# Score products in three float32r parts instead of float32, with a shifted schedule of the attention stage

## What is computed

```
scores = einsum('bhid,bhjd->bhij', Q, K) / scale
QJ     = einsum('bhid,hde->bhie', tanh(Q), J_attn)
scores = scores + lambda_attn * einsum('bhie,bhje->bhij', QJ, tanh(K))
scores = where(causal, -inf, scores)
out    = einsum('bhij,bhjd->bhid', softmax(scores), V);   x = x + out @ Wo.T + bo
```

## Time and profile before

| | |
|---|---|
| median of 3 runs | 2140.23 us (2136.80 to 2142.74) |
| the profiled execution | 2137.79 us, span 2136.1 us |
| PE busy | 1957.2 us, 92% of the span |
| DVE, ACT, POOL busy | 1246.5, 1065.7, 820.6 us |
| attention, routing with shared expert, experts (about) | 0 to 1165, to 1500, to 2136 us |
| granted PE clock, mean | 0.983 |

### The profile page before, as it was taken

The page is one execution under the profiler, slowest core; times in us unless marked ns, Lnnn a source line. Parts: engine busy times, 40 slices in busy tenths (PEclk is TensorE's granted clock), DMA queues, the critical chain, the costliest instruction groups (busy, mean ns, idle before and its releaser), DMA issues. The chain is left out here.

```text
span 2136.1 us, 48445 instructions
## 1 busy us (share of the span) xinstructions
PE 1957.2 (92%) x14755; PEld 1296.5 (61%) x14824; DVE 1246.5 (58%) x3875; ACT 1065.7 (50%) x2310; POOL 820.6 (38%) x1206
## 2 busy tenths in 40 slices
PE   2689999999999999999988999997999999999997
PEld 1345445454454544545435788886777777777776
DVE  5666667766667666776662865553445545444553
ACT  1255555555555555555552345452555555555553
POOL 4033323333323333233332037773444444444443
PEclk9799999999999999999999999999999999999999
DMA  7234443344443434434322346654863333333332
GB/s 240 60 106 117 121 136 124 110 118 119 136 130 107 122 111 140 128 114 124 100 87 79 137 134 226 223 188 150 215 167 58 57 55 55 56 55 57 54 57 34
DMA packets 156641, 246.08 MB, mean 115 GB/s; under 512 B 29408, under 2 KB 90592, under 8 KB 156480
## 3 DMA queue, kind: packets, MB, share of 16 engines
q1 hardware_dynamic: 120960, 189.24, 28.9%
q0 software_dynamic: 32064, 53.44, 12.2%
q10 hardware_dynamic: 3456, 1.34, 0.3%
HBM read 111.89 MB, written 90.50 MB: 95 GB/s over the span
## 5 line engine op out<-in xcount | busy, mean ns | idle before, releaser
L680 DVE CUSTOM_DVE_ANT_0 ps_rows<-ps_rows,maskrow 128x128 f32<-128x128 f32 (+1 forms) x1009 | 477.1, 514 | 290.9 <-PE ps_rows L525 282.2
L623 ACT ACTIVATE probs<-ps_cols 128x512 f32<-128x512 f32 (+3 forms) x1024 | 392.0, 435 | 386.7 <-PE ps_cols L536 380.1
L525 PE MATMUL ps_rows<-ks,qs 32*128 32x512 f32 x1984 | 403.1, 480 | 73.5 <-DVE mx L680 38.6
L532 PE MATMUL ps_cols<-qs,ks 32*128 32x512 f32 (+3 forms) x2048 | 418.5, 485 | 2.5 <-ACT probs L623 2.4
L1642 POOL DMA_INDIRECT out_dram<-y_e,to x135 | 216.1, 1601 | 349.4 <-DMA out_dram<-y_e,to 221.5
L799 POOL TENSOR_TENSOR pace<-eps 1x1 f32<-1x1 f32 x256 | 58.2, 227 | 747.0 <-ACT probs L623 747.0
L525 PEld LDWEIGHTS ps_rows<-ks,qs 32*128 32x128 f32 x1984 | 153.3, 184 | 268.5 <-DVE mx L680 221.9
L536 PE MATMUL ps_cols<-mT,ones_r 32*128 32x512 f32 (+3 forms) x1024 | 284.8, 550 | 0.0
L1771 DVE TENSOR_TENSOR h_lo<-ps_h,h_hi 128x512 fp32r<-128x512 f32 x135 | 93.3, 691 | 232.6 <-ACT h_hi L1746 232.6
L1740 ACT ACTIVATE sg_e<-ps_ge 128x512 f32<-128x512 f32 x135 | 80.7, 598 | 263.1 <-PE ps_ge L1664 261.0
L554 PE MATMUL ps_o<-probs,vt 128*32 128x512 f32 (+3 forms) x2048 | 192.5, 448 | 0.8 <-POOL probs L801 0.8
(11 more groups left out here) (220 smaller groups left out, 3838.9 us busy)
## 6 DMA issues: line engine op xcount, KB each, us to landing
xs_d<-zrows SPq DMA_DIRECT2D x45, 408.0 KB, 2.9
xr<-xs_d POOLq DMA_DIRECT2D x135, 136.0 KB, 3.3
whi_d<-w_sh SPq DMA_DIRECT2D x16, 768.0 KB, 3.8
w_hi<-whi_d SPq DMA_DIRECT2D x24, 512.0 KB
xn<-in_L_attn_x_dram SPq DMA_DIRECT2D x16, 512.0 KB, 5.2
ks<-k_lin SPq DMA_DIRECT2D x64, 128.0 KB, 3.0
ks<-k_tan SPq DMA_DIRECT2D x64, 128.0 KB, 3.7
qs<-q_lin SPq DMA_DIRECT2D x64, 128.0 KB, 2.4
```

The lines of the kernel that those rows point to most:

```text
L525: mm = nc.tensor.matmul(ps_rows[bank_of(row_no(g, it, h))][:, 0:(it + 1) * P], qs[at:at + STRIP, d.par, g, it * P:(it + 1) * P], ks[at:at ...
L532: nc.tensor.matmul(ps_cols[bank_of(col_no(n, s, e))][:, jt * P:S], ks[at:at + STRIP, b.par, gc, jt * P:(jt + 1) * P], qs[at:at + STRIP, b. ...
L623: nc.scalar.activation(probs[:, n % 2, 2 * (1 - s) + e, jt * P:S], ps_cols[bank_of(col_no(n, s, e))][:, jt * P:S], ACT.Exp).then_inc(exp_d ...
L680: nc.vector.tensor_tensor_reduce(out=bank, in0=bank, in1=maskrow[:, (TT - 1 - it) * P:S], scale=1.0, scalar=LOWEST, op0=ALU.add, op1=ALU.m ...
```

## The change

- Every score product becomes three float32r products (`PART_PAIRS`): of the upper parts, and of each upper with the other's lower part. The loop over parts is outermost, over rows and columns of the half. Line 536's product stays.
- The stacks hold both parts: `ks` and `qs` get a part dimension and are float32r. SP copies into the place of the lower part; POOL makes the upper part from it (a copy) and subtracts it in place, a group at a time, at `PARTS_STEPS`. PE waits for `k_parts` and `q_parts` at the first rows of each group.
- `LEAD` is 6. The pieces are in another order: k, q, qj of the first half of the heads, then of the second; all turnings "mt" for steps 2, 6, 10, 14 at place 1.
- `invert`, `normalize`, `store_rec` and `spread_rec` are each one step later.
- The staging of `wq`, `wk`, `wv` lies in `x1T` and `xres`. The shared weights are split in the prologue's step 8 into the room of the second stack, stored to memory at step 12, and loaded back into the first stack in batch 15 at step 2.

```diff
@@
 NSLOT = 2 * NT + NE - 1
 ZR = 3
 EARLY = 4
-LEAD = 8
+LEAD = 6
 STEPS = G * TT
 STRIP = 2 * HD
 PART_PAIRS = ((0, 0), (0, 1), (1, 0))
-SPLIT_STEPS = (3, 5, 8, 9, 11, 12)
+SPLIT_STEPS = (3, 8, 10, 11, 13, 14)
+PARTS_STEPS = {4: ("k", 0, 1), 5: ("k", 1, 1), 7: ("q", 0, 1), 9: ("q", 1, 1), 12: ("k", 2, 1), 15: ("q", 2, 1), 0: ("k", 3, 0), 1: ("q", 3, 0)}
 PROLOGUE, TAIL = -1, NB
 BEYOND = 1 << 14
 XW = D + 16
...
@@
 
 PIECES = [
     (0, 0, "xt", 0, 1), (0, 1, "xt", 1, 1),
-    (1, 0, "mt", 1, 0),
-    (2, 0, "k", 0, 1),
-    (3, 0, "k", 1, 1),
-    (4, 0, "q", 0, 1),
-    (5, 0, "q", 1, 1), (5, 1, "mt", 2, 0),
-    (6, 0, "qj", 0, 1),
+    (2, 0, "k", 0, 1), (2, 1, "mt", 1, 0),
+    (3, 0, "q", 0, 1),
+    (4, 0, "qj", 0, 1),
+    (5, 0, "k", 1, 1),
+    (6, 0, "q", 1, 1), (6, 1, "mt", 2, 0),
     (7, 0, "qj", 1, 1),
     (8, 0, "v", 0, 1),
-    (9, 0, "v", 1, 1), (9, 1, "mt", 3, 0),
-    (10, 0, "out", 0, -1),
+    (9, 0, "v", 1, 1),
+    (10, 0, "out", 0, -1), (10, 1, "mt", 3, 0),
     (11, 0, "out", 1, -1),
     (12, 0, "gt", 0, -1),
     (13, 0, "gt", 1, -1),
-    (14, 0, "mt", 0, 1),
+    (14, 1, "mt", 0, 1),
     (15, 0, "lg", 0, -1),
 ]
 PER_BATCH = {"xt": 2, "k": 2, "q": 2, "qj": 2, "v": 2, "mt": G, "out": 2, "gt": 2, "lg": 1}
...
@@
             nc.vector.reciprocal(rstd1[:, 0:EARLY * TT], rstd1[:, 0:EARLY * TT])
 
 
-    ks = sb("ks", [P, 2, G, S])
-    qs = sb("qs", [P, 2, G, S])
+    stack_1 = sb("stack_1", [P, 2, 2, G, S], F32R)
+    shared_0 = shared_in_stack(stack_1)
+    ks, qs = ([half[:, side] for half in (stack_0, stack_1)] for side in range(2))
     xn = sb("xn", [P, TT, D])
     xT = sb("xT", [P, 2, KT, S], F32R)
     wkp = sb("wkp", [P, 2, KT, D], F32R)
...
@@
 
     def first_rows(d, u):
 
-        return d.off == 0 and u < STEPS * HG // 2
+        return d.off == 0 and u < LEAD * HG
 
     def row_bank(d, u):
 
...
@@
             if has_rows and first_rows(d, row_no(g, it, 0)):
                 if s == 1:
                     return
-                if g == 0 and it == TT - 1:
-                    for loaded in (k_in, q_in):
-                        pe.wait_ge(loaded[0], 64)
+                if it == TT - 1:
+                    for parted in (k_parts, q_parts):
+                        pe.wait_ge(parted, (g + 1) * 2)
                 if row_no(g, it, 3) >= 6:
                     pe.wait_ge(max_done, row_no(g, it, 3) - 5)
-                for h in range(HG):
-                    at = STRIP * h
-                    mm = nc.tensor.matmul(row_bank(d, row_no(g, it, h))[:, 0:(it + 1) * P],
-                                          qs[at:at + STRIP, d.par, g, it * P:(it + 1) * P],
-                                          ks[at:at + STRIP, d.par, g, 0:(it + 1) * P], start=True, stop=True)
-                    if h % 2:
-                        mm.then_inc(rows_ready, 1)
+                for no, (kp, qp) in enumerate(PART_PAIRS):
+                    for h in range(HG):
+                        at = STRIP * h
+                        mm = nc.tensor.matmul(row_bank(d, row_no(g, it, h))[:, 0:(it + 1) * P],
+                                              qs[d.par][at:at + STRIP, qp, g, it * P:(it + 1) * P],
+                                              ks[d.par][at:at + STRIP, kp, g, 0:(it + 1) * P], start=no == 0, stop=no == 2)
+                        if no == 2 and h % 2:
+                            mm.then_inc(rows_ready, 1)
                 return
             if has_rows:
-                if g % 2 == 0 and it == TT - 1 and s == 0:
-                    for loaded in (k_in, q_in):
-                        pe.wait_ge(loaded[g // 2], (d.v + 1) * 64)
+                if it == TT - 1 and s == 0:
+                    for parted in (k_parts, q_parts):
+                        pe.wait_ge(parted, (d.v * G + g + 1) * 2)
                 w = max(last_use(row_no(g, it, 2 * s + e)) for e in range(2))
                 if w >= 0 or d.at_least(1):
                     pe.wait_ge(max_done, d.v * HEADS + w + 1)
...
@@
                 w = max(last_use(col_no(n, s, e)) for e in range(2))
                 if w >= 0 or b.at_least(1):
                     pe.wait_ge(exp_done, b.v * HEADS + w + 1)
-            if has_rows:
-                for e in range(2):
-                    h = 2 * s + e
-                    at = STRIP * h
-                    mm = nc.tensor.matmul(ps_rows[bank_of(row_no(g, it, h))][:, 0:(it + 1) * P],
-                                          qs[at:at + STRIP, d.par, g, it * P:(it + 1) * P],
-                                          ks[at:at + STRIP, d.par, g, 0:(it + 1) * P], start=True, stop=True)
-                mm.then_inc(rows_ready, 1)
+            for no, (kp, qp) in enumerate(PART_PAIRS):
+                if has_rows:
+                    for e in range(2):
+                        h = 2 * s + e
+                        at = STRIP * h
+                        mm = nc.tensor.matmul(ps_rows[bank_of(row_no(g, it, h))][:, 0:(it + 1) * P],
+                                              qs[d.par][at:at + STRIP, qp, g, it * P:(it + 1) * P],
+                                              ks[d.par][at:at + STRIP, kp, g, 0:(it + 1) * P], start=no == 0, stop=no == 2)
+                    if no == 2:
+                        mm.then_inc(rows_ready, 1)
+                if has_cols:
+                    for e in range(2):
+                        at = STRIP * (2 * (1 - s) + e)
+                        nc.tensor.matmul(ps_cols[bank_of(col_no(n, s, e))][:, jt * P:S],
+                                         ks[b.par][at:at + STRIP, kp, gc, jt * P:(jt + 1) * P],
+                                         qs[b.par][at:at + STRIP, qp, gc, jt * P:S], start=no == 0, stop=False)
             if has_cols:
-                for e in range(2):
-                    at = STRIP * (2 * (1 - s) + e)
-                    nc.tensor.matmul(ps_cols[bank_of(col_no(n, s, e))][:, jt * P:S], ks[at:at + STRIP, b.par, gc, jt * P:(jt + 1) * P],
-                                     qs[at:at + STRIP, b.par, gc, jt * P:S], start=True, stop=False)
                 for e in range(2):
                     at = STRIP * (2 * (1 - s) + e)
                     mm = nc.tensor.matmul(ps_cols[bank_of(col_no(n, s, e))][:, jt * P:S], ones_r[at:at + STRIP],
...
@@
                 maximum(b, n, 1)
                 piece(b, n, 1)
                 if piece_exists(b, -1):
-                    if n == 1:
+                    if n == 2:
                         invert(b.plus(-1), 1)
-                    if n == 5:
+                    if n == 6:
                         normalize(b.plus(-1), 1)
                 if b.at_least(0) and b.at_most(NB - 1):
-                    if n == 9:
+                    if n == 10:
                         invert(b, 0)
-                    if n == 13:
+                    if n == 14:
                         normalize(b, 0)
                 if 11 <= n < 11 + TT and piece_exists(b, -1):
                     statistics(b.plus(-1), n - 11)
...
@@
             nc.gpsimd.tensor_tensor(w_sl[:, m, half], w_st[:, m, half], w_sh[:, m, half].bitcast(F32), ALU.subtract)\
                 .then_inc(w_split, 1)
 
+        def parts_of(side, d, g):
+
+            stacked, loaded, parted = (ks, k_in, k_parts) if side == "k" else (qs, q_in, q_parts)
+            upper, lower = (stacked[d.par][:, part, g] for part in range(2))
+            pool.wait_ge(loaded[g // 2], (d.v + 1) * 64)
+            nc.gpsimd.tensor_copy(upper, lower.bitcast(F32)).then_inc(parted, 1)
+            pool.wait_ge(parted, (d.v * G + g) * 2 + 1)
+            nc.gpsimd.tensor_tensor(lower, lower.bitcast(F32), upper.bitcast(F32), ALU.subtract).then_inc(parted, 1)
+
+        def shared_parts():
+
+            pool.wait_ge(shared_in, 3 * 16)
+            for m in range(3):
+                nc.gpsimd.tensor_copy(shared_0[m][:, 0], shared_st[m]).then_inc(shared_split, 1)
+            pool.wait_ge(shared_split, 3)
+            for m in range(3):
+                nc.gpsimd.tensor_tensor(shared_0[m][:, 1], shared_st[m], shared_0[m][:, 0].bitcast(F32), ALU.subtract)\
+                    .then_inc(shared_split, 1)
+
         def batch(b):
             att = b.at_least(0) and b.at_most(NB - 1)
             for n in range(STEPS):
                 if att:
                     select(b, n)
+                if n in PARTS_STEPS and piece_exists(b, PARTS_STEPS[n][2]):
+                    side, g, rel = PARTS_STEPS[n]
+                    parts_of(side, b.plus(rel), g)
+                if b.off == PROLOGUE and n == 8:
+                    shared_parts()
+                if att:
                     if n in SPLIT_STEPS:
                         split(b, SPLIT_STEPS.index(n))
                 if n == 6 and piece_exists(b, -1):
...
@@
         assert NSLOT == (NB - 1) * ZR * ZR
         xs_z = xs_d.rearrange("(a p s) d -> a p (s d)", p=P, s=ZR)
 
-        def to_stack(d, j, stack, c, tile, done, loaded):
+        def to_stack(d, j, stacked, c, tile, done, loaded):
 
```

(23 more changed lines are left out.)

43 lines of the change are left out of this document (23 added, 20 removed).

## The result

The changed kernel takes 2263.78 us (median; 2252.89 to 2272.85) beside 2141.48 us for the kernel before on the same chip: a ratio of 1.058, with a 95% interval of 1.0537 to 1.0623. The forecast was 2168 us, slower by 28; it is slower by 122. The direction was right; the size and the range were not.

What follows compares the result with a forecast made beforehand. TensorE sets the pace: 61.0 us of work plus 7.6 of waits make a batch 68.6 us, 2.3 more. Over fifteen batches +35, with -7 before batch 0, 2137.8 becomes 2166, median 2168 us; range 2145 to 2195.

Steps and rivals of the forecast that it cites:

- step 14: PE's wait between the halves of step 14, rows of 512 with nothing between: 1.0 us a batch.
- step 15: PE's wait at step 15 for a maximum behind normalize and the last statistics on DVE: 1.1 us a batch.
- step 1: PE's wait at step 1's second half for a maximum standing behind the second xT on DVE: 1.1 us a batch.
- step 10: PE's wait at step 10 for DVE's maximum behind the negation and layer norm: 1.3 us, bounds 0 and 1.5.
- the rest: Small PE waits on ACT's mT copy and on ACT at steps 5, 0 and 12: 0.55 us a batch.
- The halves: PE's two parts of each step, paced by the wider of rows and columns: 1.08, 0.87, 0.87, 0.71 us.
- weight loads of a pass at nothing: Weight loads on PE hidden beside the pass before, costed at nothing; 2.7 us a batch if none were hidden.
- the 7 us: Prologue: six steps of rows instead of eight start batch 0 at about 80 us, -7 us (0 to -10).
- Lockstep: Rival: short column passes on PE end with the long row passes beside them, +12 us, 2180; chance 0.09.
- No change: Rival: layer norm fits under the output product, normalize and statistics overlap better, 2142; chance 0.12.
- faster: Rival: DVE runs ahead with the maxima, only ACT's waits stay, 2087; step 14 wait under 0.3 us; chance 0.16.
- Two clocks a column: Rival: float32r products on 32 rows with four strips cost two clocks a column, not one, 2320; chance 0.02.

Runs made afterwards that it cites:

- run with three waits moved: Changed kernel with step 14's turning back in the first half, statistics one step earlier and the layer norm at step 12: 2276.84 us, ratio 1.0656.
- GpSimd's load alone: Kernel before, plus the changed kernel's GpSimd copies and subtractions on buffers nobody reads, and its weight-split steps: 2160.38 us, ratio 1.0102.
- run with GpSimd's splits earlier: Fastest run: rows eight steps ahead, turnings back, layer norm and statistics spread, negation rewritten, then GpSimd's jobs moved to other steps; 2118.33 us, ratio 0.9903.
- run with fillers at steps 14 and 15: Changed kernel with eight useless matmuls a batch in batches 1 to 14, ahead of the second halves of steps 14 and 15: 2249.6 us, ratio 1.0514.
- run with three fillers: Changed kernel with useless matmuls ahead of the second halves of steps 14, 15 and 1: 2239.18 us, ratio 1.0474.
- run with the other form: Changed kernel with rows eight steps ahead, turnings back, layer norm by rows, and VectorE's first negation instruction written with two inputs: 2149.06 us, ratio 1.0041.

## Why the prediction was wrong

**The waits: right in place and in sum, single ones off by up to 0.3 us.** At the full clock, forecast and measured: step 14, 1.0 and 0.96; step 15, 1.1 and 1.42; step 1, 1.1 and 1.18; step 10, 1.3 and 1.10; the starts of steps 5, 9 and 13, 3 x 0.34 and 3 x 0.43 on ScalarE; the starts of steps 4, 8 and 12, together 1.06, with the 0.26 of step 0 just ahead of the window 1.3, forecast 1.2; the second xT, 0.3 and 0.05; the rest, 0.55 and 0.63. Within the window the sum is 7.68, forecast 7.6. That the sum fits so closely is luck: the errors cancel. The wait at step 8 for q's copies went, as forecast. The layer norm's place between its bounds (1.3 of 0 to 1.5) was chosen rightly, with two errors that cancel: in this batch the layer norm takes 3.42 us beside GpSimd (the 2.9 in the sum stands in no row), and the two instructions of the negation take 0.18 and 0.19, not 0.7. Step 15 is longer because normalize takes 1.08 us there beside GpSimd, priced at 0.61. GpSimd is busy 36.6 us a batch (36 forecast).

**The halves: mechanism right, size off.** Forecast 1.08, 0.87, 0.87, 0.71; measured 1.13 (758.79 to 759.92), 0.91, 0.89 (787.28 to 788.17) and 0.72 to 0.76 (789.54 to 790.30). One to five hundredths in 32 halves are about 1.1 of the 1.5 us by which PE's 62.47 us lie above the forecast of 61.0. At 512 columns two passes take 0.47 us (759.13 to 759.60), where 2 x 512 clocks are 0.43: so a pass costs a little more than a clock a column. The term "weight loads of a pass at nothing" (bound: 2.7 us a batch) is where the rest would go; the 0.28 us from a half's first row pass to its second, against 0.17 to its third at 384 columns, looks like that, but no run separates it. The two together put a batch at 70.15 us instead of 68.6 at the full clock: 19 to 22 us of the miss.

**The step that failed: durations at a clock taken as given.** Every term of the sum was priced at 2.4 GHz because the earlier trace rows showed a granted clock of 1.00, and "the sum is 7.6 against 5.0" was taken as a sum only. What the sum left out is what the waits do to the clock: 0.96, 1.42, 0.26, 0.20 and 1.18 us come one after the other between step 14 and step 1, and there the clock fell. The runs with fillers show it by the counter-test: with the idle time there filled, the clock holds in thirteen batches of fourteen. That is 48 us in batches 1 to 14. In batch 0 it is at 0.5 for 41 us (8 in the kernel before) and in batch 15 for 44 (14 before); the 12 us by which each of the two is longer than forecast lie there too, but were not taken apart from their other waits. What is shown is that filling these waits keeps the clock up; that their closeness counts, and not their sum over the batch, is argued from where the falls begin. No rival named the clock: all four were about the length of waits and halves.

**The prologue: the 7 us did not come, and of these 3 by the order on VectorE.** The first full half stands at 87.45 us, against 87.19 before, not at 80. Rows begin at 65.51 instead of 57.99, and then stand still on VectorE:

```profile
65.51 0.80 PE L515 MATMUL ps_rows<-stack 32*128 32x512 f32 x3
...
66.29 3.74 DVE L684 TENSOR_SCALAR xn<-xn,mv,rstd 128x256 f32<-128x256 f32 x4
...
69.95 1.39 DVE L772 BATCH_NORM_STATS2 st<-probs 128x6 f32<-128x256 f32 x4
...
71.68 0.68 DVE L697 CUSTOM_DVE_ANT_0 ps_rows<-ps_rows,maskrow 128x512 f32<-128x512 f32 x1
...
73.11 0.69 PE L515 MATMUL ps_cols<-stack 32*128 32x384 f32 x2 [5.95 <-DVE mx L697]
```

With six steps the first rows come at step 10 of the prologue, so the layer norm of its step 9 (3.74 us beside GpSimd's parts) and a set of statistics stand ahead of the first maxima on VectorE, where eight steps put the first maxima before them. I had moved PE's order and GpSimd's, and not VectorE's: the first maximum begins 6.2 us after its rows. The run with three waits moved has its layer norm at step 12, and there the same place reads:

```profile
64.69 0.69 PE L515 MATMUL ps_cols<-stack 32*128 32x384 f32 x2 [2.96 <-DVE mx L697]
```

Its batch 0 starts at 79.84 us, as forecast. Of the 7.6 us between the two runs, 3.0 are this wait on VectorE. The other 4.7 lie ahead of the first rows (65.51 against 60.76), where twelve products of v take 2.9 us in the changed kernel and 1.7 in that run; why they do is open, since the code is the same up to there.

**Behind attention, 6 us, forecast 0 (to +8 for the shared weights).** The cause is open. GpSimd's load alone has 5 of them in the kernel before (996.9 against 991.7), where no shared weight is moved, and the run with GpSimd's splits earlier has 5 less (993.3 against 998.0). But the run with fillers at steps 14 and 15, whose code is the changed kernel's from batch 15 on, has 993.4: single executions differ by as much there.

Added up, against the forecast's own parts: 19 us until batch 1 (7 of them the prologue), 67 in batches 1 to 14 (19 at the full clock, 48 from the clock), 12 in batch 15, 6 behind: 104, the 2268.5 of the span against 2164.

**The rivals.** Lockstep (2180) falls by the rows: with rows of 512 and columns of 256 the closing product starts at 787.75, ahead of the last row pass at 787.85, which was issued before it, and the half is 0.89 us. The Trainium skill ("TensorE: Matmul & The Clock Gate", The mechanism, Part 3) has matmuls start and end in program order, by which it would be 0.23 + 1792 clocks, 0.98; the measurement decides, for strips of unequal widths. "No change" had the layer norm fit under the output product: step 10 waits 1.10 us for it. The rival "faster" named its point, a wait under 0.3 us at step 14; it is 0.96. Two clocks a column is out: 1.13 us at 512 columns.

## What to carry to other kernels

Idle time of the engine that sets the pace is not only a sum. Before adding 2.6 us of waits a batch, see where they stand: here several waits of about 1 us close together cost more in clock (48 us in fourteen batches) than in waiting (14 x 2.7), and a filler without any use was worth its time. And an engine with time to spare is not free: look at what its neighbour on the same memory does in the very moment that it is given work.

## What the runs showed of the hardware

- The granted clock fell from 1.00 to 0.50 in attention with PE 90% busy over the span. Between the step 14 and the step 1 of a batch of the changed kernel no single wait is longer than 1.44 us at the full clock; PE was busy 5.64 of the 7.40 us ahead of a fall, and 1.18 of 2.10 ahead of the one in the run with three fillers. In the kernel before, batches 1 to 14, with 5.0 us of waits each spread over sixteen steps, have no fall at all; the fastest run has 6.0 us, and none either. No run keeps the sum of the waits and changes their spread alone. In the changed kernel it came back where PE had worked nearly without a wait (12.97 of 13.65 us).
- It does not hang on the products: float32 in one product and float32r in three fell alike (181 and 137 us).
- VectorE's negation of 16 columns is held until GpSimd's instruction beside it ends (run with the other form): 185 to 188 ns alone, 326 to 1395 beside GpSimd, with all 41 ends within 0.1 us of the end of a GpSimd instruction. Its median fell from 670 to 230 when GpSimd's jobs were moved off those moments. In the changed kernel itself it takes 183 in the median, and there it is the layer norm that is slow: 3.42 us in most batches, four times 0.40 where GpSimd stands still.
- With equal widths, three float32r products on 32 rows beat one float32 product at 512 columns (a half of 1.13 against 1.31 us) and lose to it at 128 (0.60 to 0.76 against 0.49).
